# A decoder kernel on one core: a stage's feed-forward weights are split beside an earlier stage, and stored

## The reference, cut to what matters

```python
# layer 0
x = x + attention(layernorm(x))            # 16 heads of 128, causal            (stage 1)
x = x + cross_attention(layernorm(x), ctx) # 16 heads of 8                      (stage 2)
y = layernorm(x); x = x + y                # residual of the feed-forward input (stage 3)
z = rmsnorm(y)                             # attention over z gives only a modulation of rank 16
m = 0.1 * tanh(att(z) @ Wo.T @ A) * (z*ln2 @ A)
h = silu((z*ln2) @ W_in.T + m @ B) * ((z*ln2) @ W_up.T)   # 256 -> 1024
x = x + h @ W_down.T
# layer 1: stage 4 (attention by running sums), stage 5 (cross attention, and a feed-forward
# 256 -> 2048 whose weights are stored as 4-bit codes)
```

## Time and profile before

| what | us |
|---|---|
| three executions | 1841.38, 1846.21, 1853.18; median 1846.21 |
| the profiled execution | 1839.15, of it the span of the trace 1837.0 |
| TensorE busy | 1634.2 (89% of the span) |
| VectorE, ScalarE, GpSimd busy | 1133.4, 844.2, 684.0 |
| stage 1 | 10.9 to 568.3 |
| stage 2 | 568.4 to 695.9 |
| stage 3: statistics, splitting, preparation | 696.5, 707.9, 720.0 |
| stage 3: attention, feed-forward | from 732.4, from 866.6 |

### The profile page before, as it was taken

The page is one execution under the profiler, slowest core; times in us unless marked ns, Lnnn a source line. Parts: engine busy times, 40 slices in busy tenths (PEclk is TensorE's granted clock), DMA queues, the critical chain, the costliest instruction groups (busy, mean ns, idle before and its releaser), DMA issues. The chain is left out here.

```text
span 1837.0 us, 32979 instructions
## 1 busy us (share of the span) xinstructions
PE 1634.2 (89%) x12606; PEld 1263.3 (69%) x12606; DVE 1133.4 (62%) x1852; ACT 844.2 (46%) x1403; POOL 684.0 (37%) x508
## 2 busy tenths in 40 slices
PE   4999999999996885798999688999998698999997
PEld 3888888888884663676888443444444475888886
DVE  6667776776776886665522868998996565111111
ACT  3555455455553663555422335555552574222222
POOL 0021211212123650900432108999995340333332
PEclk9999999999998996999999789999999898999999
DMA  3011111111112003001020100000000910000001
GB/s 100 16 61 56 43 52 57 66 40 58 51 43 87 2 2 97 10 10 27 19 101 0 38 0 0 1 1 0 1 1 1 344 39 1 1 1 1 1 0 46
DMA packets 67247, 67.73 MB, mean 37 GB/s; under 512 B 24208, under 2 KB 60560, under 8 KB 66496
## 3 DMA queue, kind: packets, MB, share of 16 engines
q1 hardware_dynamic: 67136, 66.19, 11.1%
HBM read 45.86 MB, written 19.27 MB: 35 GB/s over the span
## 5 line engine op out<-in xcount | busy, mean ns | idle before, releaser
L546 POOL TENSOR_TENSOR s_w_parts<-s_w_raw,s_w_parts 128x768 fp32r<-128x768 f32 x16 | 29.6, 1853 | 429.4 <-ACT s_w_parts L498 429.4
L1347 DVE TENSOR_TENSOR s6f_hid<-s6f_act_sb,s6f_u_ps 128x512 f32<-128x512 f32 x64 | 44.1, 688 | 218.4 <-PE s6f_u_ps L1298 218.4
L1370 POOL TENSOR_TENSOR s6f_hid_parts<-s6f_hid,s6f_hid_parts 128x512 fp32r<-128x512 f32 x64 | 82.2, 1284 | 225.4 <-ACT s6f_hid_parts L1336 225.4
L2012 POOL TENSOR_TENSOR s4b_pcs<-s4b_cs,s_p_rows 128x1024 f32<-128x1024 f32 x64 | 120.6, 1907 | 92.8 <-ACT s4b_cs L2058 89.4
L2023 POOL TENSOR_TENSOR s4b_with_re<-s4b_with_re,s4b_with_im 128x1024 f32<-128x1024 f32 x64 | 150.5, 2376 | 2.6 <-DVE s4b_with_im L1977 2.6
L2102 PE MATMUL s4b_c_ps<-s4b_pcs,const 128*128 128x512 f32 x256 | 121.6, 598 | 0.0
L422 PE MATMUL s_v_ps<-s_wv_parts,s_xnT 128*128 128x256 f32 x768 | 104.5, 286 | 11.8 <-ACT s_v L527 6.3
L481 PE MATMUL s_o_ps<-s_w_parts,s_zT 128*128 128x256 f32 x768 | 109.4, 292 | 4.1 <-DVE x_rows L585 4.1
L422 PEld LDWEIGHTS s_v_ps<-s_wv_parts,s_xnT 128*128 128x128 f32 x768 | 96.9, 191 | 17.4 <-ACT s_v L527 9.5
L1336 ACT ACTIVATE s6f_hid_parts<-s6f_hid 128x512 fp32r<-128x512 f32 x64 | 40.5, 632 | 144.3 <-PE s6f_o_ps L1318 140.8
L1318 PEld LDWEIGHTS s6f_o_ps<-s6w_parts,s6f_hid_parts 128*128 128x128 f32 x768 | 99.2, 188 | 6.8 <-issue 1.0
(11 more groups left out here) (314 smaller groups left out, 4017.2 us busy)
## 6 DMA issues: line engine op xcount, KB each, us to landing
stored_weights<-s1q_halves SPq DMA_DIRECT2D x16, 768.0 KB, 3.5
s6w_parts<-stored_weights SPq DMA_DIRECT2D x32, 384.0 KB, 7.9
s1q_packed<-in_codes SPq DMA_DIRECT2D x8, 384.0 KB, 4.5
s1q_scale<-in_scale_rows SPq DMA_DIRECT2D x8, 384.0 KB, 5.1
early_values<-s_vbd SPq DMA_DIRECT2D x1, 2176.0 KB, 11.9
s_vbd<-early_values SPq DMA_DIRECT2D x1, 2176.0 KB, 12.6
x_rows<-in_x SPq DMA_DIRECT2D x1, 2048.0 KB, 8.3
s_w_raw<-in_L_attn_W_Q SPq DMA_DIRECT2D x16, 128.0 KB, 2.2
```

The lines of the kernel that those rows point to most:

```text
L1347: nc.vector.tensor_tensor(hid[:, f % 2, :], act_sb[:, f % 2, :], u_ps[:, f % 2, :], ALU.mult) \
L1370: nc.gpsimd.tensor_tensor(hid_parts[:, f % 2, 1, :], hid[:, f % 2, :], hid_parts[:, f % 2, 0, :], ALU.subtract).then_inc(low_done, 1)
L2012: last = nc.gpsimd.tensor_tensor(pcs[:, half, n_, :].rearrange("p (k c) -> p k c", k=HK), cs[:, half, n_, :].rearrange("p (k c) -> p k c", ...
```

## The change

The three feed-forward matrices of stage 3 come in 8 pieces of 128 x 768 (both halves of W_in and W_up for 128 columns, interleaved, and a 128 x 256 piece of W_down; put so by the host). A new class `FfnWeights` works on one piece per round of stage 1: SyncE loads it, ScalarE scales the two halves by ln2 in unit 4 of the round (two activations of 128 x 256) and makes the high part in unit 6 (one copy of 128 x 768), each at lag 4, that is at the end of steps 0 and 2; GpSimd makes the low part; SyncE stores 768 KB. A new class `StoredFfn` loads the 8 split pieces and B three times at the end of SyncE's list in stage 2. Stages 2 and 3 become one (`stage_L0_cross_and_ffn`). Stage 3 no longer loads, scales or splits the big matrices; B's rows are cleared, split and subtracted in the preparation part instead of in the attention. `EarlyKeys` has scratch of its own. VectorE takes stage 3's `bn_stats` in stage 2, at lag 7.

```diff
+class FfnWeights:
+    def load(self, sp, rnd):
+        wait(sp, self.low_done, rnd)
+        sp.dma_start(self.raw..., self.ins["ffn_pieces"]...[:, bass.ds(rnd, 1), :, :]).then_inc(self.arrived, 16)
+    def store(self, sp, rnd):
+        sp.wait_ge(self.low_done, rnd + 1)
+        sp.dma_start(self.core.ffn_weights..., self.parts...).then_inc(self.stored, 16)
+    def scalar(self, u, rnd, k):
+        nc, act = self.nc, self.nc.scalar
+        if k == 4:
+            act.wait_ge(self.ln_in, 16)
+            act.wait_ge(self.arrived, 16 * rnd + 16)
+            for c in range(NC):
+                nc.scalar.activation(self.raw[:, c, :], self.raw[:, c, :], ACT.Identity, scale=self.ln[:, 1, c:c + 1]) \
+                    .then_inc(self.scaled, 1)
+        elif k == 6:
+            act.wait_ge(self.scaled, 2 * rnd + 2)
+            wait(act, self.stored, 16 * rnd)
+            nc.scalar.activation(self.parts[:, 0, :, :], self.raw[:, :, :], ACT.Copy).then_inc(self.high_done, 1)
+    def gpsimd(self, rnd):
+        nc.gpsimd.wait_ge(self.high_done, rnd + 1)
+        nc.gpsimd.tensor_tensor(self.parts[:, 1, :, :], self.raw[:, :, :], self.parts[:, 0, :, :], ALU.subtract) \
+            .then_inc(self.low_done, 1)
+
+class StoredFfn:
+    def load(self, sp):
+        for j in range(FFN_PIECES):
+            sp.dma_start(self.parts[:, j, :, :, :]..., self.core.ffn_weights[j, :, :]).then_inc(self.arrived, 16)
+        for at in (0, 32, 64):
+            sp.dma_start(self.b[at:at + 16, :], self.ins["L0_ffn_B"]).then_inc(self.b_in, 16)
...
 stage 1
             deq.load(sp, 0)
+            ffn.load_norm(sp)
+            ffn.load(sp, 0)
...
                     if slot == 0:
                         deq.load(sp, rnd)
+                    else:
+                        ffn.store(sp, rnd - 1)
+                        ffn.load(sp, rnd)
...
+                ffn.store(sp, FFN_PIECES - 1)
                 for stored in deq.stored:
                     sp.wait_ge(stored, 8 * PIECES)
+                sp.wait_ge(ffn.stored, 16 * FFN_PIECES)
...
-                                   (z_high_part, 4), (split_high, 0), (deq.scalar, 4)], unroll=8)
+                                   (z_high_part, 4), (split_high, 0), (deq.scalar, 4),
+                                (ffn.scalar, 4)], unroll=8)
...
+                def split_ffn(h, rnd, slot):
+                    if slot == 1:
+                        ffn.gpsimd(rnd)
...
-                                    (lambda j, rnd, slot: deq.gpsimd_low(j, slot), 2)])
+                                    (lambda j, rnd, slot: deq.gpsimd_low(j, slot), 2),
+                                    (split_ffn, 1)])
...
 stage 2
                 load_context(sp, 1, NT // CHUNK)
+                prefetch(sp)
...
-                run_steps(dve, U, [(shift, 3), (attended, 5)], unroll=2, head=U + 5)
+                def gather_stats(u, rnd, n):
+                    if u % 2:
+                        dve.wait_ge(added, u + 1)
+                        nc.vector.bn_stats(core.stats[:, u // 2, :], core.x[:, u // 2, :])
+
+                run_steps(dve, U, [(shift, 3), (attended, 5), (gather_stats, 7)], unroll=2, head=U + 7)
+                core.stats_ready = True
...
 stage 3
-            loads = (("wq", "WqT"), ("wk", "WkT"), ("wv", "WvT"), ("wo", "L0_ffn_Wo"), ("A", "L0_ffn_A"),
-                     ("in", "WinT"), ("up", "WupT"), ("down", "WdownT"))
+            loads = (("wq", "WqT"), ("wk", "WkT"), ("wv", "WvT"), ("wo", "L0_ffn_Wo"), ("A", "L0_ffn_A"))
...
-                for at in (0, 32, 64):
-                    sp.dma_start(w["B"][at:at + R, :], ins["L0_ffn_B"]).then_inc(w_in, 16)
...
                 nc.gpsimd.memset(a2[:, :, :], 0.0).then_inc(a2_zeroed, 1)
+                for rows in (b_rows, m_rows):
+                    nc.gpsimd.memset(rows[:].bitcast(F32), 0.0).then_inc(zeroed, 1)
+                pool.wait_ge(high_done, 1)
+                pool.wait_ge(zeroed, 2)
+                nc.gpsimd.tensor_tensor(b_rows[64:64 + R, :], stored.b[64:64 + R, :], b_high[64:64 + R, :],
+                                        ALU.subtract).then_inc(low_done, 1)
...
                 nc.scalar.activation(a2_parts[:, 0, :, :], a2[:, :, :], ACT.Copy).then_inc(a2_high, 1)
+                act.wait_ge(stored.b_in, 48)
+                act.wait_ge(zeroed, 2)
+                for at, dst in ((0, b_rows), (32, b_rows), (64, b_high)):
+                    last = nc.scalar.activation(dst[at:at + R, :], stored.b[at:at + R, :], ACT.Copy)
+                last.then_inc(high_done, 1)
...
-                for n in ("in", "up"):
-                    for c in range(NC):
-                        nc.vector.tensor_scalar(w[n][:, c, :], w[n][:, c, :], ln[:, 1, c:c + 1], None, ALU.mult)
...
-        attention16(core, "ffn", "s3a", mv, rstd, factor, w, zT, mT, beside=([high_part(n) for n in parts] + [high_rows], low_parts))
-        feed_forward(core, "s3f", zT, part_of("in"), part_of("up"), ...
+        attention16(core, "ffn", "s3a", mv, rstd, factor, w, zT, mT)
+        feed_forward(core, "s3f", zT, stored.gate, stored.up, stored.down, F, ACT.Silu, (mT, m_rows, b_rows),
+                     stats=True, early=EarlyKeys(core, room), ready=stored.ready)
```

More of the change, by code:

```diff
@@ L910, in values_of @@
             return w["values"][:, i, b, pair // 2, :, :].rearrange("p h e -> p (h e)")
-        if prefetch:
+        if prefetch and not own:
             @block.sync
@@ L1082, in weights @@
             def weights(i, rnd, k):
-                if i % 2 == 1 and i // 2 < len(beside[0]):
+                if beside and i % 2 == 1 and i // 2 < len(beside[0]):
                     beside[0][i // 2](act)
@@ L1396, in __init__ @@
         n = NT * W
-        self.raw, self.rot = rows(floats("in")[:, 0:n]), rows(floats("in")[:, n:2 * n])
-        self.spread = w["all"][:, 0:2, :].rearrange("p k n -> p (k n)")
+        scratch = room.sb("scratch", [P, 6 * n])
+        self.raw, self.rot = rows(scratch[:, 0:n]), rows(scratch[:, n:2 * n])
+        self.spread = scratch[:, 0:4 * n]
         self.kn = rows(room.sb("kn", [P, NT * W])[:, :])
@@ L1526, in stage_L0_ffn @@
         w["WoA"] = room.sb("WoA", [P, NC, R])
-        parts = {n: room.sb(n + "_parts", [P, 2, 2 * F], F32R) for n in ("in", "up", "down")}
-        w["B"] = room.sb("B", [64 + R, F])
         b_high = room.sb("b_high", [64 + R, F], F32R)
@@ L1533, in stage_L0_ffn @@
         m_rows = room.sb("m_rows", [64 + R, NT, P], F32R)
-        w["all"] = room.sb("all", [P, 3, NC * F])
-        for n, (name, c) in enumerate((("in", NC), ("up", NC), ("down", F // P))):
-            w[name] = w["all"][:, n, :].rearrange("p (c n) -> p c n", c=c)
         high_done, low_done, zeroed = room.sems("high_done", "low_done", "zeroed")
@@ L1626, in _ @@
                 nc.vector.tensor_copy(w["WoA"][:, :, :], wa_ps[:, :, 0:R])
-        def high_part(name):
-            def part(act):
-                nc.scalar.activation(parts[name][:, 0, :], flat(name), ACT.Copy).then_inc(high_done, 1)
-            return part
-        def high_rows(act):
-            act.wait_ge(zeroed, 2)
-            for at, dst in ((0, b_rows), (32, b_rows), (64, b_high)):
-                last = nc.scalar.activation(dst[at:at + R, :], w["B"][at:at + R, :], ACT.Copy)
-            last.then_inc(high_done, 1)
@@ L1640, in low_parts @@
-        def low_parts(pool):
-            for rows in (b_rows, m_rows):
-                nc.gpsimd.memset(rows[:].bitcast(F32), 0.0).then_inc(zeroed, 1)
-            for n, name in enumerate(parts):
-                pool.wait_ge(high_done, n + 1)
-                nc.gpsimd.tensor_tensor(parts[name][:, 1, :], flat(name), parts[name][:, 0, :], ALU.subtract) \
-                    .then_inc(low_done, 1)
-            pool.wait_ge(high_done, len(parts) + 1)
-            pool.wait_ge(low_done, len(parts))
-            pool.wait_ge(zeroed, 2)
-            nc.gpsimd.tensor_tensor(b_rows[64:64 + R, :], w["B"][64:64 + R, :], b_high[64:64 + R, :], ALU.subtract) \
-                .then_inc(low_done, 1)
-            pool.wait_ge(low_done, len(parts) + 1)
@@ L1654, in flat @@
-        def flat(name):
-            return w[name][:, :, :].rearrange("p c n -> p (c n)")
-        def part_of(name):
-            return lambda part, c, f: parts[name][:, part, c * F + f * P:c * F + (f + 1) * P]
-        attention16(core, "ffn", "s3a", mv, rstd, factor, w, zT, mT, beside=([high_part(n) for n in parts] + [high_rows], low_parts))
-        feed_forward(core, "s3f", zT, part_of("in"), part_of("up"),
-                     lambda part, f: parts["down"][:, part, f * D:(f + 1) * D], F, ACT.Silu, (mT, m_rows, b_rows),
-                     stats=True, early=EarlyKeys(core, room, w))
@@ L2380 @@
                                      .reshape(8, P, D).transpose(1, 0, 2)),
+    "ffn_pieces": lambda i: np.stack(
+        [np.concatenate([i["L0_ffn_" + n].T[c * P:(c + 1) * P].reshape(P, 8, P) for n in ("W_in_base", "W_up_base")], 2)
```

(1 more changed line is left out.)

62 lines of the change are left out of this document (49 added, 13 removed).

## The result

The changed kernel takes 1839.35 us (median of 20 runs, 1834.41 to 1841.65), the kernel before 1845.57 us (median of 20, 1839.85 to 1858.52). The ratio is 0.9962, 95% interval 0.995 to 0.9975: 7.0 us faster (4.6 to 9.2 by the interval); the two medians are 6.2 us apart. The forecast was 1843.3 us, range 1829 to 1855. The profiled execution of the changed kernel took 1839.2 us, its span is 1837.4 us, against 1837.0 us before. So the two traces are equally long although the medians are not, and the first thing to settle is where in them the change can be seen at all.

What follows compares the result with a forecast made beforehand. TensorE's in-order stream, made to wait by late ScalarE copies, was taken to bound stage 1, and idle TensorE stretches stage 3. Losses of 15.8 and gains of 18.7 us netted -2.9, giving 1843.3 us from median 1846.21, range 1829 to 1855.

Steps and rivals of the forecast that it cites:

- Scaling: Stage 1, unit 4: two ScalarE activations per round delay the scores matmul by 0.91 us, eight rounds, +7.3 us.
- High part: Stage 1, unit 6: a ScalarE copy of 0.83 us delays the values copy TensorE waits for, seven times, +5.8 us.
- GpSimd in stage 1: GpSimd's new subtraction, 1.85 us a round in stage 1, falls in its idle time and holds nothing: 0.
- Rival 2: Stage 1: the new GpSimd subtraction holds VectorE's multiply 1.85 us in eight rounds; net +11.9, 1858 us; chance 0.10.
- End of stage 1: The awaited last feed-forward store lands after VectorE's end, near 569.0: +1.3 us (0 to 2.9).
- Stage 2: Loads of split weights cost 0; VectorE's 16 added statistics instructions cost only the last one, +0.4 us.
- Start of stage 3: Without the statistics and with six SyncE issues instead of twelve, splitting starts at 700.1, not 707.93: -7.8 us.
- Preparation: Stage 3: GpSimd's clearings hold VectorE's scaling of A, so the mT matmuls start later: +1.0 us (0 to 2.7).
- Attention: Stage 3: with GpSimd's large subtractions gone, VectorE's multiply of 11.43 us no longer stalls: -10.9 us.
- rival 4: Stage 3's attention: the 11.43 us stall is not GpSimd's and stays; +8.0, 1854 us; chance 0.05.
- Rival 3: Stage 1: longer waits lower TensorE's clock, 2.9 us each, seven times; net +17.4, 1864 us; chance 0.05.
- The sum: All terms over stages 1 to 3: 15.8 us lost, 18.7 gained, net -2.9 us; chance 0.55.

Runs made afterwards that it cites:

- a3: The changed kernel without ScalarE's two scalings per round in stage 1: stage 1 takes 564.0 us, 5.6 less.
- a2: The changed kernel with ScalarE's scalings and high part moved in its order to just ahead of the exponent: 1832.84 us, ratio 0.9935.
- c3: The kernel before with only GpSimd's order in stage 1 turned, the dequantiser's subtraction first: 1840.60 us (one run), stage 1 547.5 us.
- c1: The changed kernel with scalings ahead of the exponent, last feed-forward store earlier, GpSimd's dequantiser subtraction first, high part left in place: 1815.82 us, ratio 0.9856.
- d1: The changed kernel with VectorE's 16 statistics instructions put back from stage 2 to the start of stage 3: 1843.19 us.
- a4: The kernel before with GpSimd's three subtractions in stage 3's attention replaced by clearings of the same outputs: 1833.6 us (one run).
- a5: The kernel before with a GpSimd wait for its own last subtraction between the three in stage 3's attention: 1834.07 us (one run); timed again, ratio 0.9962.
- c2: The kernel before with GpSimd's stage 1 order turned and a wait between its three stage 3 subtractions: 1826.50 us, ratio 0.992.

## Why the prediction was right, step by step

- **Scaling**: forecast +7.3, shown 5.6 by taking it away. ScalarE was late, as said, and passed on what the two scalings occupied. The rows give them 0.89 us, but the q copy starts 0.80 us behind them (284.82, 285.62): in the record an instruction's end overlaps the next one's start. Eight times 0.80 is 6.4, and the scores wait grew by 6.3. I had multiplied the length and not the distance between starts.
- **High part**: forecast +5.8, measured +5.0 in the wait rows (0.71 for 0.83; from start to start it is 0.73, 301.37 to 302.10). No run takes the high part alone away; what is left of stage 1 in a3, +6.7 us, is these 5.0 and the end of the stage. The size was nearly right; the reason, "it is late, not waiting", held only for the copy itself. The exponent three instructions earlier waits for VectorE, which GpSimd holds. That is why moving the high part bought nothing (a2) and moving GpSimd's subtraction took away the whole wait (c3, c1).
- **GpSimd in stage 1**: forecast 0, right for this place: its subtraction takes 1.88 us at 302.27, and the multiply that I feared for takes 941 to 954 ns. It was close: GpSimd ends at 304.15 and the multiply starts at 304.27. Rival 2 named the right mechanism and the wrong instruction; it decides once the high part is done sooner.
- **End of stage 1**: forecast +1.3, measured +1.6 (VectorE idle 2.27 against 0.70), of it 1.2 ahead of the barrier, the store's part.
- **Stage 2**: forecast +0.4, measured +0.8 between the profiles and +1.4 against d1: the statistics inside the loop are not quite free, though in c1, which has them, the stage takes 127.8 us.
- **Start of stage 3**: forecast -7.8, measured -7.9, and split by d1 as argued. Against the median of the seven kernels with the old code it would be -7.1.
- **Preparation**: forecast +1.0, measured 0. The scaling of A was held, but 0.5 us rather than to the end of both clearings, and ScalarE would have come to A no sooner. This is the one term that failed in kind.
- **Attention**: forecast -10.9, measured -10.3; a4 and a5 show that it was GpSimd's reads, so rival 4 is out. The size held because the profile that I forecast from is also the one that I compare with; c3 shows the same code 7.8 us slower. Rival 3 is out by the clock of 1.00 in stage 1.
- **The sum**: forecast -2.9, the parts give -4.8: the costs of stage 1 came 2.1 us lower and that of the preparation 1.0, and 1.2 us of small terms went the other way. The time lies well inside the stated range, and the mechanisms are the forecast ones but for the preparation and the reason behind the high part. The gain itself was under-forecast: 2.9 us lie outside the interval of the ratio, 4.6 to 9.2. The difference of 15.8 lost and 18.7 gained is small beside its terms, and the range of 26 us is wide beside it, so that the range held says little of the sum; the parts say more. Of the 3.95 us between 1843.3 and 1839.35, 1.9 are in the parts and 0.6 between the two medians of the kernel before; for the other 1.4 I have no cause.

Open is why the three subtractions kept the multiply out to the end, while in a2 VectorE's addition got in between two adjoining subtractions (293.19 and 294.99). In the code a wait stands between the instructions in both places, in the loop against a count that grows with the round, between the three against a fixed count that is met long before; whether that makes the difference was not tried. The 20 runs of the kernel before spread over 18.7 us and those of the changed one over 7.2; whether it is this stall that varies is not shown. Not tried either is a kernel with c2's order and wait and with the statistics in stage 2. By d1's 5.3 us it would come to about 1821 us, an estimate, without any work moved to stage 1.

## What to carry to other kernels

Before work is moved away from a stall, look at what makes the stall: a wait of GpSimd for its own last subtraction was worth as much as moving three of them, with their loads and stores, into another stage. Compare an instruction's median length with its shortest; one that mostly takes 2.6 us and can take 0.94 is being held, and the engine that "is late" further down the chain may only be passing that on. And forecast from several executions where there are any: stages that nobody touched differed by 5 us between profiles, as much as the change was worth, and in c3 a part with the same code took 7.8 us longer where only an earlier stage had been changed.

## What the runs showed of the hardware that I had not expected

- GpSimd instructions that read, issued back to back, held a VectorE instruction with two SBUF inputs through all of them (11.43 us over three), and a gap of 0.15 us between them was enough to let it in (2.47 us). It is no rule for every such pair: in stage 1 an addition got in between two adjoining ones (2.57 us).
- A clearing with nothing right behind it did not hold such an instruction (0.28 us beside it). With a reading instruction right behind, it was held through both, 6.04 us, and with another clearing and three reading ones behind, through all of them, 15.60 us.
- The hold goes both ways: GpSimd's subtraction of 1.84 us took 2.56 us when VectorE's addition was in first.
